# Cross-attention on one core: the order of a step's products, of the next group's layer norm and of the slot statistics

## The reference

```python
q = layernorm(x) @ Wq + bq;  k = ctx @ Wk + bk;  v = ctx @ Wv + bv        # 16 heads of 64
p = softmax(where(mask, -1e30, q k^T / 8))                                # 1024 x 154 a head
x = x + (p v) @ Wo + bo
xn = layernorm(layernorm(x), norm_g, norm_b)
se = layernorm(slot_embeds, slot_g, slot_b) * scale                       # 16 x 64 slots of 256
logits = xn se^T                                                          # dispatch and combine softmaxes
...                                                                       # expert FFNs on the slots
x = x + combine @ eout
```

## Time and profile before

| | us |
|---|---|
| median of 3 runs | 632.36 (631.05 to 634.88) |
| the profiled execution | 632.31 |
| its span | 630.6 |
| busy in the span: PE / DVE / ACT / POOL | 576.8 / 481.6 / 399.8 / 323.9 |

### The profile page before, as it was taken

How to read it: one execution, slowest core, us unless ns; L and a number is a source line. 1 busy time by engine, 2 the same in 40 slices (tenths; PEclk the granted TensorE clock), 3 DMA queues, 4 the chain that set the end, 5 groups by cost and what they waited for, 6 DMA issues and landing times.

```text
span 630.6 us, 11863 instructions
## 1 busy us (share of the span) xinstructions
PE 576.8 (91%) x3888; PEld 512.8 (81%) x3888; DVE 481.6 (76%) x1335; ACT 399.8 (63%) x1054; POOL 323.9 (51%) x324
## 2 busy tenths in 40 slices
PE   7697999999979999999979987899979999999998
PEld 3576999999969999899967765788846777779998
DVE  3666777787786988787666998898798999965553
ACT  3747959687774959688653545466476666655563
POOL 5817345344444344443446978666256999930000
PEclk9888999999998999999989999799959999999999
DMA  7700000000020000000001433041048788813542
GB/s 237 218 2 1 2 2 2 1 2 1 2 83 3 2 2 1 2 0 3 1 2 67 167 137 162 2 143 64 1 131 296 241 266 273 281 47 117 177 168 75
DMA packets 34828, 53.36 MB, mean 85 GB/s; under 512 B 6125, under 2 KB 21425, under 8 KB 34769
## 3 DMA queue, kind: packets, MB, share of 16 engines
q1 hardware_dynamic: 34769, 52.61, 24.5%
HBM read 42.12 MB, written 10.49 MB: 83 GB/s over the span
## 4 chain that ended last, share of the span: by engine, by line
PE 56%; DVE 19%; ACT 14%; issue 6%; POOL 4%; DMA 0%; SPq 0%; DVEq 0%; POOLq 0%; ACTq 0%
PE ps L1223 7%; PE ps L1354 7%; PE ps L1309 7%; ACT expo L666 6%; PE ps L1284 5%; PE ps L1209 4%; PE ps L1331 4%; PE ps L1255 3%; DVE expo L896 3%; DVE pT_low L916 3%; DVE qT_low L790 2%; PE ps L1164 2%; PE ps L1343 2%; PE ps L1211 2%; ACT pT_high L680 2%
## 5 line engine op out<-in xcount | busy, mean ns | idle before, releaser
L666 ACT ACTIVATE expo<-expo,nmin 128x154 f32<-128x154 f32 x256 | 106.2, 417 | 58.6 <-DVE nmin L896 57.5
L532 POOL TENSOR_TENSOR prob<-expo,prec 128x512 f32<-128x512 f32 x64 | 67.1, 1048 | 116.7 <-DVE prec L907 114.6
L1181 PE MATMUL ps<-kbd,qT_high 128*128 128x308 f32 x256 | 72.1, 322 | 2.5 <-DVE nmin L896 1.7
L916 DVE TENSOR_TENSOR pT_low<-ps,pT_high 128x512 fp32r<-128x512 f32 (+1 forms) x96 | 54.3, 591 | 19.9 <-ACT pT_high L680 19.5
L896 DVE CUSTOM_DVE_ANT_0 expo<-ps,maskb 128x154 f32<-128x154 f32 x256 | 66.9, 311 | 0.0
L593 POOL TENSOR_TENSOR wkq_low<-w_raw,wkq_high 128x1024 fp32r<-128x1024 f32 x16 | 50.9, 3181 | 25.6 <-ACT wkq_high L624 25.6
L1181 PEld LDWEIGHTS ps<-kbd,qT_high 128*128 128x128 f32 x256 | 46.6, 190 | 5.3 <-DVE nmin L896 5.1
L680 ACT CAST pT_high<-ps 128x512 fp32r<-128x512 f32 (+1 forms) x96 | 46.0, 511 | 7.6 <-PE ps L1193 5.4
L803 DVE TENSOR_TENSOR w_gu_low<-w_raw,w_gu_high 128x1024 fp32r<-128x1024 f32 x18 | 45.4, 2532 | 4.5 <-ACT w_gu_high L624 4.4
L666 ACT ACTIVATION_READ_ACCUMULATOR expo<-expo,nmin 128x1 f32 x256 | 48.4, 189 | 0.0
L790 DVE SCALAR_TENSOR_TENSOR qT_low<-ps,bq_c,qT_high 128x256 fp32r<-128x256 f32 x64 | 30.6, 480 | 16.2 <-ACT qT_high L602 16.1
(11 more groups left out here) (215 smaller groups left out, 1842.3 us busy)
## 6 DMA issues: line engine op xcount, KB each, us to landing
logits_dram<-lsb SPq DMA_DIRECT2D x16, 512.0 KB, 2.6
w_raw<-in_L_ffn_Wg_dram SPq DMA_DIRECT2D x16, 512.0 KB, 4.2
w_raw<-in_L_ffn_Wu_dram SPq DMA_DIRECT2D x16, 512.0 KB, 4.5
w_raw<-in_L_ffn_Wd_dram SPq DMA_DIRECT2D x16, 512.0 KB, 4.2
lraw<-logits_dram SPq DMA_DIRECT2D x16, 512.0 KB, 3.5
out_dram<-outb SPq DMA_DIRECT2D x16, 128.0 KB, 1.7
x<-in_x_dram SPq DMA_DIRECT2D x1, 1792.0 KB, 10.6
wraw<-in_L_xattn_Wk_dram SPq DMA_DIRECT2D x2, 512.0 KB, 4.7
```

The source lines that it names most:

```text
L532: pool.tensor_tensor(prob[:, n % 2, :, heads, :], expo[:, n % 2, pp, :, :, 0:P], prec[:, n % 2, pp].unsqueeze(3).to_broadcast([P, 2, 2, P] ...
L666: ins = act.activation(row, row, ACT.Exp, scale=-1.0, bias=nmin[:, n % 2, pp, j, h:h + 1], accum_out=psums[:, n % 2, pp, j, h:h + 1])
L916: dve.tensor_tensor(pT[1][0:rows, n % 2, 2 * t:2 * t + tiles], ps[0:rows, NS + k % NT, 0:tiles * 2 * P].rearrange("p (t n) -> p t n", t=ti ...
L1181: ins = pe.matmul(dst, qT[s][:, n % 2, pp, j * P:(j + 1) * P], kbd[:, b, m, p, :], start=(r == 0), stop=(r == 2))
```

## The change

Four things are edited. In STEP, Q0 moves from behind T0 to ahead of LN, PV0 and T0. LN (and with its condition `norm` XN) moves from step 1 of a group to step 2, and within the step behind Q0. SA becomes five events, SA 0 to SA 3 with the statistics of two slot tiles each, and SA 4 with the scalings and aggregates (and POOL's rstd); they stand ahead of S00 of steps 17 to 21, and SB(0) to SB(7) ahead of S00 of steps 22 to 29. A semaphore se_stats joins the statistics to the aggregates.

```diff
-STEP = "R1 LN S00 S01 PV0 T0 Q0 R0 PV1 XN Q1 S10 T1 T2 Y0 Y1 S11 xT0 xT1"
+STEP = "R1 S00 S01 Q0 LN PV0 T0 R0 PV1 XN Q1 S10 T1 T2 Y0 Y1 S11 xT0 xT1"
...
-        norm, result = q == 1 and g + 1 < groups, q == 1 and g >= 1
+        norm, result = q == quads - 2 and g + 1 < groups, q == 1 and g >= 1
...
-    norms = [("SA",)] + [("SB", t) for t in range(ST)]
+    norms = [("SA", k) for k in range(ST // 2 + 1)] + [("SB", t) for t in range(ST)]
...
-            elif ev[0] == "SA":
+            elif ev == ("SA", ST // 2):
                 pool.wait_ge(se_var, 1)
...
             elif ev[0] == "SA":
-
+                k = ev[1]
                 dve.wait_ge(d_se, 64)
-                for t in range(ST):
-                    dve.bn_stats(sst[:, t], se[:, t])
-                dve.tensor_scalar(sg_b[:], sg_b[:], sc_b[:], None, ALU.mult)
-                link(dve.tensor_scalar(sb_b[:], sb_b[:], sc_b[:], None, ALU.mult))
-                for t in range(ST):
-                    ins = dve.bn_aggr(smv[:, t], sst[:, t])
-                ins.then_inc(se_var, 1)
+                if k < ST // 2:
+                    for t in (2 * k, 2 * k + 1):
+                        ins = dve.bn_stats(sst[:, t], se[:, t])
+                    ins.then_inc(se_stats, 1)
+                else:
+                    dve.tensor_scalar(sg_b[:], sg_b[:], sc_b[:], None, ALU.mult)
+                    link(dve.tensor_scalar(sb_b[:], sb_b[:], sc_b[:], None, ALU.mult))
+                    dve.wait_ge(se_stats, ST // 2)
+                    for t in range(ST):
+                        ins = dve.bn_aggr(smv[:, t], sst[:, t])
+                    ins.then_inc(se_var, 1)
```

More of the change, by code:

```diff
@@ L341, in program @@
     dve_step, pool_step = sem("dve_step"), sem("pool_step")
-    se_var, se_rstd, se_ready = sem("se_var"), sem("se_rstd"), sem("se_ready")
+    se_stats, se_var, se_rstd, se_ready = sem("se_stats"), sem("se_var"), sem("se_rstd"), sem("se_ready")
     x2_centered, x2_ready, x2_high, x2_low = sem("x2_centered"), sem("x2_ready"), sem("x2_high"), sem("x2_low")
```

## The result

The changed kernel takes 649.7 us (median of 4, 645.4 to 652.5) where the kernel before takes 631.7 in the same runs: ratio 1.0285, 95% interval 1.0251 to 1.0318. It is 18 us slower. The execution that was profiled is the quickest of the four, 645.4, with a span of 643.6, 13.0 above that of the earlier trace rows; so the profile shows 13 of the 18, and the rest has to be found in executions that were not profiled.

The account below looks back on a forecast made before the run. Attention was taken to be bound by a 7.20 us cycle through PE, ACT and DVE, not PE's work. Group changes 18.7, less 4.8 and 2.0 for slot work, plus 0.1, gave +12.0 on 632.31: 644.3, range 627 to 651.

Parts of the forecast that it names:

- Ordinary steps: Attention steps away from group changes: Q0's move leaves the cycle through PE, ACT and DVE at 7.22 against 7.20; cost 0.
- Steps 2 and 3: Where the next group comes in: Q0 waits for xT, XN delays DVE's train; +2.8 a group in six groups.
- The first group: Attention's first group change: step 1 has no Y and loses LN and XN, POOL is free earlier; +1.9.
- Slot statistics: Spreading SA removes step 17's long stop, gain 4.8; moving the SB normalizations four steps on, gain 2.0.
- The clock: PE's clock around stops in steps 2 and 3: assumed to hold at 2.4 GHz; +1.6 if a drop hits Q0 and PV0.
- rival 4: The forecast's slowdown, plus PE's clock falling in most groups: up to 7 x 1.6 more, 655; chance 0.12.
- Rival 1: Q0 fills PE's gap ahead of PV0 and PE sets the pace: 623.5, with half the fill 629.5; chance 0.20.
- Rival 2: Group change costs half, as ACT and DVE recover more in steps 3 and 0: 1.4 a group, 635.5; chance 0.18.

Follow-up runs that it names:

- the filled version: Six overwritten bf16 products of 512 columns put ahead of step 3's Q0, in PE's wait for xT1, against the changed kernel: 644.4 us, ratio 1.020.

## Why the prediction was right, point by point

- **The result.** 649.7 lies in the range, 627 to 651, near its end; the sign and the likeliest cause were as forecast. The forecast of 644.3 was 5 us short. Its sum left out the clock; beside the version in which the clock is kept (644.4, 13.3 above the kernel before) its +12.0 is 1.3 short.
- **Ordinary steps cost nothing.** Right: 7.22 worked out, 7.23 measured. PE's stop moved to T2 as said (21 waits of 0.3 to 0.4 for T0's low half). The wait of S products on DVE's minimum, also announced, is not in the list of waits; a gap of 0.3 ahead of S01 stands in PE's timeline and not in the list. That moving T0's copy on ACT then shortened the step by the 0.2 that the same sum gives makes luck unlikely.
- **Steps 2 and 3.** Step 1 at 12.9: measured 12.74. Step 2 at 9.7: 9.59, with a wait of 1.47 for xT where 1.6 was said. Step 3 at 6.9: 7.12. The +2.8 a group is what the profile shows (36.65 and 36.67 against 33.86 in the second to the fourth group). The parts were each somewhat off and cancelled: XN waited 0.2 to 0.5 for rstd, 1.9 in six groups, not 0.4 each, and step 3 gave back 0.1 and not 0.3. That Q0's wait is most of the loss, and not merely beside it, is shown by putting Q0 back in step 3 alone: of the 2.8 a group 1.7 go.
- **The first group.** +1.9 was said; from its step 2 on it is +2.8 like the others (step 2 alone 9.55), so POOL's being free earlier, the 0.4 of the prediction, gave nothing. Ahead of it the profiled execution is 2.8 quicker, but the version with only the statistics spread was 1.9 quicker there too, with the same instructions in that stretch, so most of this is no effect of the change. How much is left for the lost LN stays open.
- **Slot statistics.** -4.8 and -2.0 were said for the change as a whole. In the changed kernel step 17 is 12.73 and step 21 12.75, the same as every other step 1: right. Alone, with LN still in step 1, the spreading gained only 3.8, since slot work and LN met in steps 21 and 25 (13.60 and 13.59). That normalizations beside POOL's chain in step 2 would cost 0.3 in two groups was not foreseen.
- **The clock.** This is the term that was off in size, put at nothing: "I assume that 2.4 holds", with rival 4 at 0.12 for a clock that falls in most groups. It falls at five of seven group changes in one profile, at two in the other. The price, 1.6 a time, was about right: 1.4 in the windows above. The two profiles lose 2.9 and 6.6 by it, not the 11 of rival 4; the filled version, which has none, is 5 to 7 quicker by the medians (644.4 against 649.7 and 651.2). So the new order's longer steps, less what the slot statistics gain, explain about 13 of the 18, and the clock the other 5. That the measured time lies inside the range owes something to the range's upper end, which was set by this rival and not by the forecast's own sum. The Trainium skill, "TensorE: Matmul & The Clock Gate", section "HAM oscillation — how this bites in real kernels", has a wait that returns with every tile send the array to half rate each time. Its waits are for a DMA and last some 3 to 5 us. The waits here are of 1.5 at most, and the trace agrees in that the array falls to half rate behind them, but at two or five of seven, not each time.
- **Rival 1,** that Q0 fills the gap, asked for PE to set the pace. It did not: ordinary steps stayed at 7.2. The versions with Q1 moved show PE can do a step in 6.8, but only by taking work out of DVE's train.
- **Rival 2,** that ACT and DVE recover and a group costs half, asked for 1.4 a group; 2.8 was measured.

## What to carry to other kernels

Before an item is moved into a gap on one engine, add up the cycle that makes the gap, across all engines in their new orders: here it was 7.2 before and after. And ask of an item that occurs in every step whether it has the same inputs in every step; here one step in four has an input that is made just before it, and these seven places cost 16 of 18 us. A short wait that comes back can cost the clock on top, and can be told from the queue's cost by filling it.

## What the runs showed that I had not expected

- The clock fell at two group changes in one profiled execution of the changed kernel and at five in the other. The fall comes after PE had stood for 0.2, 0.3 and 1.5, in some groups and not in others of the same execution; seven waits of up to 1.3, in the version with only Q0 moved, brought none in its profile.
- The times of the changed kernel spread from 645.1 to 653.5, those with 1.5 us of useless products in each wait from 644.0 to 645.8. The clock at the group changes is only part of this. Of the 5.9 between the two profiled spans of the changed kernel (643.6 and 649.5) it explains 3.7; 3.1 lie behind attention's last PV0 (305.4 against 308.5), in work that the change doesn't touch, and that part scatters from 305 to 311 in the profiles of all versions.
- POOL is idle for more than 60% of an ordinary step (2.73 busy of 7.23) and still held PE up for 12.0 in one version, through the place of R1 in the order.
- Two operations of 0.48 on DVE, both of slot normalization, go with POOL's 128x2 operations beside them taking 0.30 and 0.44 instead of 0.20. The changed kernel, the filled one, the one with Q0 back in step 3 and the one with only LN and XN moved all show it in their steps 2 with a slot normalization. What the engines share there was not tried by itself.
